# Selective scan of a four-layer hybrid network: every fourth state's product with its c rows on GpSimd, the decay rows kept in SBUF two deep, the residual sum moved to the delta stage

## The reference, cut to what matters

```python
def _mamba_block(x, ...):                       # D = 256 channels, N = 16 states
    residual = x
    ...                                         # norm, projection, convolution, silu -> x1, g
    dbc = x1 @ dbc_W + dbc_b
    delta, Bm, Cm = (dbc[..., :DTR], dbc[..., DTR:DTR + N], dbc[..., DTR + N:])
    delta = jax.nn.softplus(delta @ dup_W + dup_b)
    A_disc = jnp.exp(delta[..., None] * A)
    B_x = delta[..., None] * Bm[:, :, None, :] * x1[..., None]
    def step(hc, inp):
        a, b = inp
        hc = a * hc + b
        return (hc, hc)
    _, hs = jax.lax.scan(step, h0, (Ad_t, Bx_t))
    y = jnp.einsum('tbdn,btn->btd', hs, Cm)
    y = jax.nn.silu(g) * y
    out = y @ out_W + out_b
    return out + residual
```

## Time and profile before

| | us |
|---|---|
| median of 3 runs | 5742.93 (5742.36 to 5756.35) |
| the profiled execution, its own time | 5715.51 |
| its span | 5713.8 |
| scan stage of the first block, 172 to 632 us of the span | 460 |
| scan stage of the second block, 4285 to 4520 us | 235 |
| VectorE busy in 172 to 632 | 435.5 |
| GpSimd busy there | 301.6 |
| TensorE busy there | 353.6 |
| ScalarE busy there | 271.6 |

### The profile page before, as it was taken

One profiled execution on the slowest core, in us unless ns is written; L12 is line 12 of the kernel. 1 busy time (PEld: TensorE's weight loads), 2 busy tenths in 40 slices (PEclk: granted clock), 3 DMA queues, 4 the chain that ended last, 5 costly groups with the idle time before them and its releaser, 6 DMA issues. The chain is left out here.

```text
span 5713.8 us, 91311 instructions
## 1 busy us (share of the span) xinstructions
PE 4713.6 (82%) x33501; PEld 2077.9 (36%) x33596; DVE 3783.7 (66%) x4596; ACT 3163.8 (55%) x6002; POOL 1683.8 (29%) x1468
## 2 busy tenths in 40 slices
PE   5677668998579977799778998589867799799999
PEld 2233223443233336333353333256422344333344
DVE  6899658886589943899448882677539710799400
ACT  5656444766448853488535885444466422488621
POOL 0666315886032215322252220000006400222100
PEclk7899888999789989899898998799989999799999
DMA  0000001111021125211242110000000000111100
GB/s 28 0 1 1 4 28 55 44 45 29 10 72 50 49 74 168 74 49 51 91 150 71 48 52 15 2 10 2 4 10 0 21 0 0 40 38 38 43 0 15
DMA packets 120296, 211.54 MB, mean 37 GB/s; under 512 B 34982, under 2 KB 71442, under 8 KB 118484
## 3 DMA queue, kind: packets, MB, share of 16 engines
q1 hardware_dynamic: 110580, 182.00, 10.4%
q10 hardware_dynamic: 4320, 15.73, 0.9%
q0 software_dynamic: 4992, 8.41, 0.5%
HBM read 153.93 MB, written 52.00 MB: 36 GB/s over the span
## 5 line engine op out<-in xcount | busy, mean ns | idle before, releaser
L958 ACT ACTIVATE l_core_probs<-l_core_ps_scores_b 128x512 f32<-128x512 f32 (+3 forms) x3840 | 1610.1, 508 | 584.6 <-PE l_core_ps_scores_b L866 419.4
L1060 DVE TENSOR_REDUCE l_core_chunk_max<-l_core_ps_scores_a 128x2 f32<-128x1024 f32 (+3 forms) x1280 | 1253.2, 1020 | 84.3 <-PE l_core_ps_scores_a L851 48.9
L866 PE MATMUL l_core_ps_scores_b<-l_q_rows_sb,l_k_rows_sb 64*128 64x512 bf16 (+3 forms) x3840 | 948.7, 333 | 39.9 <-ACT l_core_probs L958 16.6
L851 PE MATMUL l_core_ps_scores_a<-l_k_rows_sb,l_q_rows_sb 64*128 64x512 bf16 (+3 forms) x3840 | 741.2, 345 | 104.0 <-DVE l_core_chunk_max L1060 44.9
L1009 POOL TENSOR_SCALAR_AFFINE_SELECT l_core_probs<-l_core_probs 128x512 f32<-128x512 f32 x512 | 325.8, 636 | 1174.4 <-ACT l_core_probs L958 1169.7
L881 PE MATMUL l_core_ps_acc<-l_core_probs,l_v 128*9 128x512 f32 (+3 forms) x6144 | 648.8, 494 | 15.9 <-ACT l_core_out_sums L932 8.6
L866 PEld LDWEIGHTS l_core_ps_scores_b<-l_q_rows_sb,l_k_rows_sb 64*128 64x128 bf16 x3840 | 304.4, 94 | 702.4 <-ACT l_core_probs L958 614.1
L1060 DVE TENSOR_REDUCE l_core_neg_max<-l_core_ps_scores_a 128x2 f32<-128x256 f32 (+3 forms) x640 | 493.3, 819 | 95.7 <-PE l_core_ps_scores_a L811 93.5
L1931 POOL TENSOR_TENSOR l_scan_bx<-l_xs,l_scan_b_rows 128x1024 f32<-128x1024 f32 x192 | 452.3, 2356 | 224.2 <-DVE l_scan_states L1941 217.9
L1941 DVE TENSOR_TENSOR_SCAN l_scan_states<-l_scan_ps_decay,l_scan_bx 128x1024 f32<-128x1024 f32 x192 | 439.7, 2290 | 40.8 <-POOL l_scan_bx L1931 15.3
L979 POOL TENSOR_TENSOR l_core_probs_decayed<-l_core_probs,l_decay 128x1536 f32<-128x1536 f32 (+2 forms) x160 | 394.0, 2487 | 145.9 <-ACT l_core_probs L958 145.9
(11 more groups left out here) (323 smaller groups left out, 7761.4 us busy)
## 6 DMA issues: line engine op xcount, KB each, us to landing
l_slots_weights<-m_both_dram SPq DMA_DIRECT2D x78, 512.0 KB, 4.6
l_q_rows_sb<-l_q_rows SPq DMA_DIRECT2D x128, 96.0 KB
l_k_rows_sb<-l_k_rows SPq DMA_DIRECT2D x128, 96.0 KB
l_heads_out<-l_core_out_sums SPq DMA_DIRECT2D x300, 32.0 KB
l_q_rows<-l_proj_parts SPq DMA_DIRECT2D x36, 256.0 KB
l_k_rows<-l_proj_parts SPq DMA_DIRECT2D x36, 256.0 KB
l_q_rows_sb<-l_q_rows SPq DMA_DIRECT2D x128, 64.0 KB
l_k_rows_sb<-l_k_rows SPq DMA_DIRECT2D x128, 64.0 KB
```

The lines of the kernel that those rows point to most:

```text
L851: mm = nc.tensor.matmul(slot[:, i, 0:w], qs[n % 3][rows, p, qt * P:(qt + 1) * P], ks[n % 3][rows, p, c * NT:c * NT + w], start=True, stop= ...
L866: mm = nc.tensor.matmul(pb[m % 3][:, 0:w], ks[n % 3][rows, p, kt * P:(kt + 1) * P], qs[n % 3][rows, p, q0:q0 + w], start=True, stop=not diag)
L958: nc.scalar.activation(pt[:, ts % RP, j, 0:w], pb[m % 3][:, 0:w], ACT.Exp, scale=scale).then_inc(b_free, 1)
L1060: nc.vector.tensor_reduce(to, pa[e % 2][:, :, 0:width_a(qt, c)], AX.X, ALU.max, negate=True).then_inc(a_free, 1)
```

## The change

In the scan stage:

- The decay rows, two deep, go to SBUF. Their place is `xn`, which is free there and is cut into four parts of 1024: two for decay, one for a copy of the c rows (`cs`), one for the product (`hp`). ScalarE may now write decay(q) when scan(q - 2) is done.
- Of every four states, the second (q % 4 == 1, `apart`) has its product with the c rows on GpSimd (`states_c`), not on VectorE. ScalarE copies its c row from PSUM to SBUF first (`copy_c`), and TensorE adds that product up two steps later than the others.
- `bx` is three deep where it was two; the copy of the b rows is three deep where it was four, and its copy stands one step later in ScalarE's queue.
- Waits are counted apart for the two kinds: `near(q)` counts the states whose product is on VectorE, `far(q)` the others.

Since `xn` is overwritten in the scan stage, the sum x + xn moves: it was VectorE's first instruction of the output stage, and is GpSimd's first instruction of the delta stage. The diff, cut to its core:

```diff
@@ ssm_delta
             @block.gpsimd
             def _(pool):
+                if residual:
+                    nc.gpsimd.tensor_tensor(net.x[:, :], net.x[:, :], net.xn[:, :], ALU.add)
                 with pool.Fori(0, TILES // 2) as i:
@@ ssm_scan
-    R, RS = 2, 4
+    R, RS, RB = 2, 4, 3
+    apart = lambda q: q % 4 == 1
+    near = lambda q: q - (q + 2) // 4
+    far = lambda q: (q + 2) // 4
-        bx = sb("bx", [P, R, S])
+        bx = sb("bx", [P, RB, S])
-        pa = ps("decay", [P, S])
+        spare = net.xn[:, :].rearrange("p (r t) -> p r t", r=4)
+        pa, cs, hp = spare[:, 0:2, :], spare[:, 2, :], spare[:, 3, :]
@@ tensor
                 def c_rows(q):
-                    if q:
-                        pe.wait_ge(hc_done, q)
+                    if q and apart(q - 1):
+                        pe.wait_ge(c_copied, far(q))
+                    elif q:
+                        pe.wait_ge(hc_done, near(q))
...
-                for q in range(Q):
+                for q in range(Q + 1):
                     if q + 3 < Q:
                         b_rows(q + 3)
-                    c_rows(q)
-                    if q:
+                    if q < Q:
+                        c_rows(q)
+                    if q >= 3 and apart(q - 3):
+                        add_up(q - 3)
+                    if q and not apart(q - 1):
                         add_up(q - 1)
@@ scalar
+                def copy_c(q):
+                    act.wait_ge(c_ready, q + 1)
+                    if far(q):
+                        act.wait_ge(hp_done, far(q))
+                    nc.scalar.activation(cs, pc[:, :], ACT.Copy).then_inc(c_copied, 1)
                 def decay(q):
-                    if q:
-                        act.wait_ge(scanned, q)
-                    nc.scalar.activation(pa[:, :], delta[:, h, b * S:(b + 1) * S], ACT.Exp,
+                    if q >= 2:
+                        act.wait_ge(scanned, q - 1)
+                    nc.scalar.activation(pa[:, q % 2, :], delta[:, h, b * S:(b + 1) * S], ACT.Exp,
...
-                for q in range(1, Q):
-                    decay(q)
-                    if q + 2 < Q:
-                        copy_b(q + 2)
-                    if q >= NS and q % NS == 1:
+                for q in range(2, Q + 3):
+                    if q < Q:
+                        decay(q)
+                    if 3 <= q + 1 < Q:
+                        copy_b(q + 1)
+                    if apart(q - 2):
+                        copy_c(q - 2)
+                    if q > NS and q % NS == 2:
                         take(q // NS - 1)
@@ gpsimd
+                def states_c(q):
+                    pool.wait_ge(c_copied, far(q) + 1)
+                    pool.wait_ge(scanned, q + 1)
+                    if far(q):
+                        pool.wait_ge(far_summed, far(q))
+                    nc.gpsimd.tensor_tensor(hp, hs[:, q % RS, :], cs, ALU.mult).then_inc(hp_done, 1)
                 for q in range(Q):
                     pool.wait_ge(bs_done, q + 1)
-                    if q >= R:
-                        pool.wait_ge(scanned, q - R + 1)
+                    if q >= RB:
+                        pool.wait_ge(scanned, q - RB + 1)
...
+                    if q >= 3 and apart(q - 3):
+                        states_c(q - 3)
@@ vector
-                    nc.vector.tensor_tensor_scan(hs[:, q % RS, :], pa[:, :], bx[:, q % R, :], 0.0, ALU.mult,
+                    nc.vector.tensor_tensor_scan(hs[:, q % RS, :], pa[:, q % 2, :], bx[:, q % RB, :], 0.0, ALU.mult,
                                                  ALU.add).then_inc(scanned, 1)
...
                 for q in range(Q):
                     scan(q)
-                    if q:
+                    if q and not apart(q - 1):
                         times_c(q - 1)
@@ ssm_output
             @block.vector
             def _(dve):
-                if residual:
-                    nc.vector.tensor_tensor(x[:, :], x[:, :], xn[:, :], ALU.add).then_inc(added, 1)
-                    dve.wait_ge(added, 1)
                 dve.sem_inc(free, 2)
```

More of the change, by code:

```diff
@@ L1710, in _, with ssm_delta @@
                 convolve(B - 1)
-def ssm_delta(net, tag, H, low_rank, a_is_log, xs, delta, bcp, dtb, dbb, acol, w_dbc, w_dt):
+def ssm_delta(net, tag, H, low_rank, a_is_log, xs, delta, bcp, dtb, dbb, acol, w_dbc, w_dt, residual):
     nc = net.nc
@@ L1871, in add_up @@
                     b, h, n = place[q]
-                    pe.wait_ge(hc_done, q + 1)
+                    if apart(q):
+                        pe.wait_ge(hp_done, far(q) + 1)
+                    else:
+                        pe.wait_ge(hc_done, near(q) + 1)
                     if n == 0 and q:
```

47 lines of the change are left out of this document (26 added, 21 removed).

## The result

| | before | after |
|---|---|---|
| median | 5742.65 us (5741.69 to 5756.35, 4 runs) | 6002.41 us (5996.31 to 6004.3, 4 runs) |
| ratio after to before | | 1.0449, 95% interval 1.0436 to 1.0462 |
| profiled execution, its own time | 5715.51 | 6001.13 |

The change makes the kernel 259.8 us slower. The forecast was 6015 within 5985 to 6100, with slower at 0.90.

A forecast was written before the change was run, and what follows sets the result against it. The prediction took VectorE's queue as the bound. Scan stages +273 us and the residual sum's move -1 gave +272, taking the profiled 5715.5 to 5987.5; with 27.4 for the median, 6015, range 5985 to 6100.

The forecast's parts named there:

- The exclusion: Scan stages: scans with two SBUF inputs and GpSimd operations block each other for whole instructions; 80% with alternation, 6015 us.
- Decay in SBUF: Scan stages: both scan inputs now in SBUF, so four states take 19.8 us instead of 13.9, 283 us more.
- rival 1: Scan stages: the scan doesn't exclude GpSimd and the kernel gets faster, gain 71 us at most, 5683 us; chance 9%.
- the floor: Scan stages: lowest cost of four states, every held operation shortened, 19.5 us; +259 us in all.
- The ceiling: Scan stages: highest cost of four states, every operation at full length, 21.0 us; +331 us in all.
- Alternation: Scan stages: VectorE gets in after one GpSimd operation even when GpSimd has its next ready; assumed in the 19.8 us.
- rival 3: Scan stages: GpSimd keeps VectorE out until its ring is full, four states take 21.9 us, 6116 us; chance 3%.
- rival 2: Scan stages: TensorE's clock falls and stays down, TensorE becomes the bound, +350 us, 6092 us; chance 8%.
- TensorE's order: Scan stages: TensorE's sums change order, which has no cost at nearly 5 us a state.
- The take's stalls: Scan stages: ten waits of VectorE for a late decay when sums are taken out vanish, -10 us.
- The residual sum: Moved from VectorE in the output stage (-4.1 us) to GpSimd in the delta stage (+3): net -1 us.
- the worse case: Delta stage: the small L1790 already waits for GpSimd's residual sum, everything behind shifts, the stage loses 3 to 3.5 us.

The follow-up runs named there:

- e3: The changed kernel with decay rows two deep in PSUM and b rows loaded by broadcast DMA from DRAM: 5626.17 us, ratio 0.9848 to the kernel before.
- e4: e3 with only its two decay rows put in SBUF, as in the changed kernel: 5973.76 us, ratio 1.0454 to the kernel before.
- e2: The kernel before with decay rows in SBUF two deep and the residual sum moved, all products on VectorE: 5920.15 us, ratio 1.0363.
- e9: e3 with all 192 products with c rows on VectorE again: 5666.99 us, ratio 0.9917 to the kernel before.
- e5: The kernel before with ScalarE's take of a token's sums queued one state later: 5731.34 us, ratio 0.9994.

## Why the prediction was right, step by step

**The exclusion** (the step "Decay in SBUF") is what the time went into: shown by e3 against e4, and by e2. It was read from three lines of other stages, and it carried over to the scan, whose speed of 2.2 ns an element might have left room. It did not: rival 1 was wrong.

**Its size** is the term that was off. I took 19.8 us for four states, from the floor of 19.5 and a little for scans that find bx by semaphore. The rows give 19.51, the floor itself: those scans exist (613.06), but the gap before them lies under GpSimd's hold, and GpSimd, always with the next operation in its queue, loses nothing. That is 48 x 0.29 = 14 us too much in the sum. It is near the 12.6 us between 6015 and 6002.4, but not the whole account: by the stages the sum of 272 stands against 264.2, 8 us. The other part is a term that the sum put at nothing, the ends of the two scan stages (under **The clock**, below). The ceiling (every hold at full length, 21.0) is excluded for this kernel: a held scan needs 2.14 us after GpSimd's end, as the 2.13 worked out from the earlier trace rows said. In e2, where GpSimd's operation is never the one held, it keeps its 2.36.

**Alternation** held (7.56 us for two scans in a row, one GpSimd operation before each), so rival 3 did not occur. The fifth GpSimd operation of a group comes where the next scan still waits for its own bx: two of GpSimd's run one behind the other after the scan that ends at 610.81, before the scan of 613.06 gets in.

**The clock** (rival 2) occurred in part. The granted clock fell from 0.98 to 0.84 and 0.82 in the scan stages, but TensorE was busy for only 412.8 of 630 us, so it did not become the bound. The row of the product with c (the only instruction of VectorE that needs TensorE) has 2.3 us of waiting for it, at two places of 144, and these are the two ends of the scan stages:

```profile
L1986 DVE TENSOR_TENSOR l_scan_states_c<-l_scan_states,l_scan_ps_c_rows 128x1024 f32<-128x1024 f32 x144 | 171.3, 1190 | 2.3 <-PE l_scan_ps_c_rows L1875 2.3
```

The rival's price rested on a clock that stays at the lower level; it went between the two levels (1.2 and 2.4 GHz), and in steady running the slower matmuls fitted under the holds. At the end of a scan stage no hold covers them. Timeline of the end of the first block's scan stage, before and then after, VectorE's last scan, TensorE's last sums and ScalarE's take:

```profile
623.51 2.29 DVE L1941 TENSOR_TENSOR_SCAN l_scan_states<-l_scan_ps_decay,l_scan_bx 128x1024 f32<-128x1024 f32 x1
...
631.04 1.02 ACT L1910 ACTIVATE l_xs<-l_scan_ps_y 128x1024 f32<-128x1024 f32 x1 [7.57 <-PE l_scan_ps_y L1876]
```

```profile
794.04 7.54 DVE L1978 TENSOR_TENSOR_SCAN l_scan_states<-x_norm,l_scan_bx 128x1024 f32<-128x1024 f32 x2
...
803.59 3.53 PE L1889 MATMUL l_scan_ps_y<-l_scan_states_c,ident 128*128 128x512 f32 x4
806.95 1.88 PE L1889 MATMUL l_scan_ps_y<-x_norm,ident 128*128 128x512 f32 x4
808.67 1.88 PE L1889 MATMUL l_scan_ps_y<-l_scan_states_c,ident 128*128 128x512 f32 x4
...
810.58 1.02 ACT L1932 ACTIVATE l_xs<-l_scan_ps_y 128x1024 f32<-128x1024 f32 x1 [14.74 <-PE l_scan_ps_y L1889]
```

From the end of the last scan to the end of the take it is 6.3 us before and 10.0 after, and in the second block 6.3 and 10.9: 8.4 us together. Twelve matmuls stand there in place of eight (before, 3.60 us from 627.41), since GpSimd's last product is summed late, and the granted clock is 0.71 in 801 to 811 us where it was 1.00 in 625 to 632. The sum said that TensorE's order has no cost; that is right in steady running and wrong at these ends. With the 14 us too much for the groups, the two errors partly cancel in the forecast.

**What bounds the kernel before** was a wrong reading that cost the forecast nothing. "VectorE's queue is the bound, with no gap" is not what e9 shows: 0.16 us in each state was a wait for the decay, and the 1.27 from product to scan is 1.11 and 0.16. In the sum as made both lie under GpSimd's hold. In rival 1 the error would have counted: without the exclusion four states take 12.12 (e3), not 12.65, and the gain is 86 us, beyond the 71 that it gave as the most.

**The take's stalls** (-10) vanish in the changed kernel, as said; e5 shows that on their own, in the kernel before, they are worth 6, not 10.

**The residual sum** was -1 and is -2.0 by the stages: the delta stage +2.6 where I took +3, the output stage -4.6 where I took -4.1. The mechanism is the one that I put as the worse case: the small L1790 already waits, for 6.69 us, until GpSimd is done at 112.0, and everything behind shifts.

**From the sum to the median.** I added 27.4 us for the offset of the profiled execution. After, that execution (6001.13) lies 1.3 us under its median (6002.41): the offset was not a property of the kernel. The stage differences sum to 264.2, the medians differ by 259.8, and the two profiled executions by 285.6, of which some 20 us lie in stages that the change doesn't touch. The choice did no harm, since 5987.5 + 27.4 is the same 6015 as the median of before plus the 272 of the sum.

## What to carry to other kernels

Before moving an operand from PSUM to SBUF to gain depth, count the SBUF inputs of the VectorE instruction that reads it: with a second one, it and GpSimd's operations that read SBUF (tensor products here) exclude each other, and what two engines did side by side becomes a sum (here 13.9 to 19.5 us for four states). If the depth is wanted, free room in PSUM for it, as e3 does: the same depth and the same moved product then gain 86 us. And a scan that starts 0.03 us after its input lands is waiting for it, even if the profile prints no wait: compare the hand-over with the same pair elsewhere.

## What the runs showed of the hardware that I had not expected

- A GpSimd fill of 128x1024 f32 lies inside a scan with two SBUF inputs, both at their usual length (0.95 and 2.28 us), while a GpSimd product of the same size is held and holds (3.28 and 3.28).
- A VectorE instruction of 128x32 on one SBUF input, written in place, 0.18 us alone, stood for 6.69 us under GpSimd's product of 4096 elements. A fill on VectorE (L1785, 1.76 us) beside the same product was not held. The Trainium skill (SBUF — State Buffer, Who interferes with whom) names `tensor_scalar`, which L1790 is, among the VectorE operations that can enter a mode with two ports and so contend with GpSimd; the 6.69 us agree.
- Three of ten equal waits of TensorE (1.38 us) in e5 were followed by a sum of which most ran at the lower clock (granted 0.53 to 0.61), 3.07 to 3.65 us for four matmuls, the other seven by one of 1.95 or 1.96.
- Broadcast DMAs of 512 KB for each state moved 163 (e9) and 174 GB/s (e3) beside the scans, at a mean busy share of the DMA engines of 0.47 and 0.51, and e3's scans and products kept their durations (2279 and 1196 ns).
